# A Mamba block before a mixture of experts on one core: delta spread by 64-row products, padded few-row products, and 26 products of constants a unit on TensorE

## The reference, cut to what matters

```
h = layernorm(x) * gamma + beta
u, z = split(h @ in_proj_w.T)                        # 256 channels each
uc = silu(causal_conv(u, 4 taps) + conv_b)
dt, B, C = split(uc @ x_proj_w.T, [64, 80])          # 64, 16 and 16 columns
delta = softplus(dt @ dt_proj_w.T + dt_proj_b)       # 256 channels
state[d, n] = exp(delta[d] * A[d, n]) * state[d, n] + delta[d] * uc[d] * B[n]   # per time step
y[d] = sum_n state[d, n] * C[n] + uc[d] * D[d]
x = layernorm(x + (y * silu(z)) @ out_proj_w.T + x)
p, e = top2(softmax(x @ Wg + bg))
out = layernorm(x + sum_k p_k * (gelu(x @ W1[e_k] + b1[e_k]) @ W2[e_k] + b2[e_k]))
```

## Time and profile before

| what | value |
|---|---|
| median of 3 runs | 893.62 us (892.45 to 897.2) |
| the profiled execution, its own time | 891.96 us |
| its span, first to last instruction | 890.2 us |
| mean granted clock of TensorE | 0.764 |
| DVE busy | 687.3 us (77% of the span) |
| PE busy | 678.5 us (76%) |
| POOL busy | 530.7 us (60%) |
| ACT busy | 423.3 us (48%) |

### The profile page before, as it was taken

One profiled execution on the slowest core, in us unless ns is written; L12 is line 12 of the kernel. 1 busy time (PEld: TensorE's weight loads), 2 busy tenths in 40 slices (PEclk: granted clock), 3 DMA queues, 4 the chain that ended last, 5 costly groups with the idle time before them and its releaser, 6 DMA issues. The chain is left out here.

```text
span 890.2 us, 12242 instructions
## 1 busy us (share of the span) xinstructions
PE 678.5 (76%) x2905; PEld 311.1 (35%) x2905; DVE 687.3 (77%) x1350; ACT 423.3 (48%) x884; POOL 530.7 (60%) x526
## 2 busy tenths in 40 slices
PE   3768989878778988878888976878631998899920
PEld 2322222222222322222232221212221888888820
DVE  2167788989998897899889899999732677777754
ACT  3537458357465534735655453324110555455424
POOL 5124546745687757677676677867863455455433
PEclk9885867877987776787797666556555899999975
DMA  3074455565376855547465465655003666666646
GB/s 82 0 202 106 95 127 133 121 152 131 82 189 172 196 135 134 122 115 172 105 142 124 112 142 118 161 120 123 24 27 91 166 177 170 176 168 178 181 128 175
DMA packets 60390, 117.37 MB, mean 132 GB/s; under 512 B 8817, under 2 KB 37297, under 8 KB 52257
## 3 DMA queue, kind: packets, MB, share of 16 engines
q1 hardware_dynamic: 56000, 107.60, 49.4%
q0 software_dynamic: 4320, 8.99, 3.1%
HBM read 100.21 MB, written 16.35 MB: 131 GB/s over the span
## 5 line engine op out<-in xcount | busy, mean ns | idle before, releaser
L532 POOL TENSOR_TENSOR hc<-hs,Crep 128x1024 f32<-128x1024 f32 x128 | 300.1, 2355 | 188.2 <-PE bank L759 102.0
L1295 DVE TENSOR_TENSOR_SCAN hs<-bank,state,flow 128x512 f32<-128x512 f32 x256 | 314.6, 1268 | 58.5 <-ACT bank L1061 53.2
L1061 ACT ACTIVATE bank<-bank,negA 128x512 f32<-128x512 f32 x256 | 165.1, 662 | 253.4 <-PE bank L749 242.0
L749 PE MATMUL bank<-delta,sel 32*128 32x512 f32 x512 | 195.0, 839 | 83.3 <-DVE hs L1295 83.2
L1285 DVE TENSOR_TENSOR flow<-flow,bank 128x2048 f32<-128x2048 f32 x63 | 142.7, 2265 | 0.0
L749 PEld LDWEIGHTS bank<-delta,sel 32*128 32x128 f32 x512 | 50.8, 237 | 212.8 <-DVE hs L1295 145.4
L1189 ACT ACTIVATE flow<-bank,b1T 128x128 f32<-128x128 f32 x284 | 81.1, 369 | 79.8 <-PE bank L926 77.6
L759 PE MATMUL bank<-hc,kc 128*32 128x512 f32 x512 | 91.2, 795 | 6.1 <-POOL hc L532 6.1
L698 PE MATMUL bank<-hT,wtapT 128*128 128x512 f32 x128 | 88.9, 822 | 6.9 <-issue 4.9
L926 PE MATMUL bank<-flow 128*128 128x128 f32 x568 | 83.0, 291 | 14.0 <-issue 9.1
L641 POOL DMA_INDIRECT results<-flow,idn x71 | 69.9, 984 | 33.2 <-issue 31.4
(11 more groups left out here) (180 smaller groups left out, 774.8 us busy)
## 6 DMA issues: line engine op xcount, KB each, us to landing
flow<-du_d SPq DMA_DIRECT2D x63, 1024.0 KB, 7.1
flow<-L_ffn_W SPq DMA_DIRECT2D x71, 256.0 KB
xg<-xs SPq DMA_DIRECT2D x71, 66.0 KB
hs<-results SPq DMA_DIRECT2D x16, 256.0 KB, 4.8
du_d<-du SPq DMA_DIRECT2D x28, 128.0 KB, 3.1
xin<-L_attn_x SPq DMA_DIRECT2D x8, 256.0 KB, 3.1
out<-hc SPq DMA_DIRECT2D x8, 256.0 KB, 2.5
results<-flow,idn POOLq DMA_INDIRECT x71
```

The costliest lines, as they stand in the source:

```text
L532: nc.gpsimd.tensor_tensor(hc[:, Q % 2, two, :], hs[:, Q % 2, two, :], Crep[u % 3][:].unsqueeze(1).broadcast_to([P, 2, T]), ALU.mult).then_ ...
L749: ins = nc.tensor.matmul(dbank[i][:], sel[32 * i:32 * i + 32, q % 4, :], delta[u % 2][32 * i:32 * i + 32, q // 4, :])
L1061: nc.scalar.activation(dbank[G % 4][:], dbank[G % 4][:], ACT.Exp, scale=negA[:, ch:ch + 1]).then_inc(s_ex, 1)
L1295: nc.vector.tensor_tensor_scan(hs[:, Q % 2, j, :], dbank[G % 4][:], flow[Q % 3][:, j, :], state[:, Q // QUADS % 2, Q % QUADS, j:j + 1], AL ...
```

## The change

1. `spread_pair` takes 64 rows of delta for each product in place of 32. sel grows from 4 to 2 x 4 matrices, one set for the even and one for the odd groups of 32 rows, with zeros in the rows of the other group. The pair of banks now holds groups 0 and 2, then 1 and 3, so the order of scans within a quad becomes 0, 2, 1, 3 (`ORDER`), and POOL takes tiles 0 and 2, then 1 and 3.
2. `spread_c`, `spread_b` (32 rows) and `proj_dt` (64 rows) use all 96 rows of xdbl, with zeros in the stationary operand where the rows aren't wanted.
3. `spread_b` moves from g=29, ahead of x_proj of unit j+2, to the end of g=31.
4. `c_evac` moves on ACT from g=6 to g=5, ahead of `one_plus` (an activation over 128 x 1024).
5. `keep_busy`: for units j = 1 to 5, at g = 3, 15, 19, 23, 25 and 27, PE issues 4, 3, 6, 3, 4 and 6 products of constant bfloat16 matrices (ones, 128 x 128 by 128 x 512) into the front bank that is filled next. Ahead of them it waits until the fill that was in this bank has been drained: at g=3 by ACT's Relu of the first half of `proj_dt`, at g=19 by `residual` on DVE.
6. The zeros of sel are set by DVE in place of POOL, and DVE also zeroes the unused rows of bcs and wdtT. POOL sets one more constant.

```diff
+ORDER = (0, 2, 1, 3)
+KEPT_BUSY = {3: (4, "dt1", 1), 15: (3, "out", -1), 19: (6, "u1", 2), 23: (3, "z0", 2), 25: (4, "xn", -1), 27: (6, "xn", -1)}
...
-        sel = sb("sel", [P, 4, P])
+        sel = sb("sel", [P, 2, 4, P])
-        wdtT = sb("wdtT", [RANK, HALVES, P])
+        wdtT = sb("wdtT", [XP, HALVES, P])
+        idle_rhs = sb("idle_rhs", [P, T], BF16)
...
 # POOL
-                two = slice(2 * pair, 2 * pair + 2)
+                two = slice(pair, 4, 2)
...
-            link(nc.gpsimd.memset(sel[:], 0.0))
+            pool.wait_ge(s_zero, 6)
             for p in range(4):
-                rows = sel[32 * p:32 * p + 32, :, :].rearrange("r m (n c) -> r m n c", c=CH)
+                rows = sel[32 * p:32 * p + 32, p % 2, :, :].rearrange("r m (n c) -> r m n c", c=CH)
...
+            link(nc.gpsimd.memset(idle_rhs[:], 1.0))
...
 # PE
-            pe.wait_ge(s_k, 8)
+            pe.wait_ge(s_k, 7)
+            pe.wait_ge(s_zero, 6)
...
-                nc.tensor.matmul(o[:], bcs[RANK:XP, 1, :], xdbl[u % 2][RANK:XP, :]).then_inc(s_ff, 1)
+                nc.tensor.matmul(o[:], bcs[:, 1, :], xdbl[u % 2][:]).then_inc(s_ff, 1)
...
-                nc.tensor.matmul(o[:], wdtT[:, h, :], xdbl[u % 2][0:RANK, :]).then_inc(s_ff, 1)
+                nc.tensor.matmul(o[:], wdtT[:, h, :], xdbl[u % 2][:]).then_inc(s_ff, 1)
...
-                nc.tensor.matmul(Brep[:], bcs[RANK:XP, 0, :], xdbl[u % 2][RANK:XP, :]).then_inc(s_br, 1)
+                nc.tensor.matmul(Brep[:], bcs[:, 0, :], xdbl[u % 2][:]).then_inc(s_br, 1)
...
-                q, j = r // 2, 2 * (r % 2)
-                for i in (j, j + 1):
-                    ins = nc.tensor.matmul(dbank[i][:], sel[32 * i:32 * i + 32, q % 4, :],
-                                           delta[u % 2][32 * i:32 * i + 32, q // 4, :])
+                q, odd = r // 2, r % 2
+                for i in range(2):
+                    rows = slice(64 * i, 64 * i + 64)
+                    ins = nc.tensor.matmul(dbank[2 * odd + i][:], sel[rows, odd, q % 4, :], delta[u % 2][rows, q // 4, :])
...
+            def keep_busy(newest, times):
+                drained(pe, newest - 1)
+                for _ in range(times):
+                    nc.tensor.matmul(fbank[(newest + 1) % 2][:], ones[:], idle_rhs[:])
...
-                    if g == 29 and late:
-                        spread_b(j + 1)
...
+                        if g == 31:
+                            spread_b(1)
...
+                    if late and g == 31:
+                        spread_b(j + 1)
+                    if early and g in KEPT_BUSY:
+                        times, what, ahead = KEPT_BUSY[g]
+                        keep_busy(fill_of(j + ahead, what), times)
...
 # ACT
-                ch = tile_of(g // 4, g % 4)
+                ch = tile_of(g // 4, ORDER[g % 4])
...
                         if g == 5:
+                            c_evac(j + 1)
                             one_plus(j + 1)
-                        if g == 6:
-                            c_evac(j + 1)
...
 # DVE
             front_stats(0)
+            nc.vector.memset(sel[:], 0.0).then_inc(s_zero, 1)
+            nc.vector.memset(bcs[0:RANK], 0.0).then_inc(s_zero, 1)
+            nc.vector.memset(wdtT[RANK:XP], 0.0).then_inc(s_zero, 1)
...
-                Q, j = G // 4, G % 4
+                Q, j = G // 4, ORDER[G % 4]
```

More of the change, by code:

```diff
@@ L959, in setup @@
                 nc.scalar.copy(wxpT[:].rearrange("p h c -> p (h c)"), bank[3][:, 0:2 * XP]).then_inc(s_pe, 1)
-                nc.scalar.copy(wdtT[:].rearrange("p h c -> p (h c)"), bank[3][0:RANK, 256:512]).then_inc(s_pe, 1)
+                nc.scalar.copy(wdtT[0:RANK].rearrange("p h c -> p (h c)"), bank[3][0:RANK, 256:512]).then_inc(s_pe, 1)
                 nc.scalar.copy(b1T[:], bank[4][:, 32:64]).then_inc(s_pe, 1)
@@ L1288, in scan @@
             def scan(G):
-                Q, j = G // 4, G % 4
+                Q, j = G // 4, ORDER[G % 4]
                 dve.wait_ge(s_ex, G + 1)
-                if j == 0:
+                if G % 4 == 0:
                     dve.wait_ge(s_bu, Q + 1)
@@ L1400, in _ @@
             nc.vector.tensor_copy(run[:], base).then_inc(s_zero, 1)
-            dve.wait_ge(s_zero, 4)
+            dve.wait_ge(s_zero, 7)
             second_h()
```

## The result

| | changed kernel | kernel before, same chip |
|---|---|---|
| median | 857.28 us (855.64 to 859.91, 4 runs) | 894.91 us (892.45 to 897.2, 4 runs) |
| ratio | 0.9583, 95% interval 0.9545 to 0.9621 | 1 |
| the profiled execution | 859.91 us, span 858.1 | 891.96 us, span 890.2 |
| mean granted clock | 0.872 | 0.764 |

The account below looks back on a forecast made before the run. DVE was taken to bound the units, with 53.2 us of waits for ACT's late decays to win. 29.2 + 5.2 + 1.9 + 0.5 - 4.8 = 32.0 us off 891.96 gave 860.0, median 861.5, range 847 to 884.

Parts of the forecast that it names:

- start, up to the first scan: Before PE's first convolution: POOL's memset of sel leaves the chain it waits for, 0.5 us gained.
- unit 0: Unit 0, wide pairs without constants: half of the 10.3 us of waits besides ACT's silu, 5.2 us gained.
- units 1 to 5, less POOL's meetings: DVE's waits there give 29.2 of 36.9 us; 4.8 lost as `one_hots` is held by POOL, half of four times.
- unit 6: Its longest DVE wait, 1.9 us, gone with the later `spread_b`.
- The signs: DVE's ACT waits about 13 us, units 1 to 5 clock over 0.9, units 68, scan 30's 3.17 gone, over-2-us records.
- 64-row pairs at 1.13 us, padding at nothing: On PE, a 64-row pair costs the same 1.13 us as a 32-row pair at 2.4 GHz; 96 rows cost nothing.
- What goes with a low clock: Narrow products keep PE's clock low; inferred from two stretches, both 81% busy, with clocks 0.80 and 0.50.
- Rival C: Busy time decides the clock: wide pairs do nothing, filled gaps do all; 864.5 us, chance 0.10.
- the move of `spread_b`: At the end of a unit, before scan 30: worth 0.6 us at 1.2 GHz, 3.17 at 2.4 GHz.
- B: In each unit the clock falls before step 19's products and stays low to its end; 879 us, chance 0.15.
- D: The clock stays as it is; the moves give 5.4 us, which POOL takes back; 892 to 893 us, chance 0.11.
- E: PE becomes the bound in units 1 to 5, from 0.47 us per constant product; 906 us, chance 0.09.

Follow-up runs that it names:

- the moves: Kernel before with only B spread later, C copied earlier, new scan order and sel zeros by DVE; no wide pairs, padding or constants: 889.43 us, ratio 0.9954.
- `one_hots` early: Changed kernel with `one_hots` moved from step 0 of the next unit to step 29: 853.39 and 855.33 us; without constants 848.66 us.

## Why the prediction was right

**What bounds the kernel.** Right: the fall of DVE's waits for late decays was the whole gain. They fell by 35.9 us (53.2 to 17.3), DVE's busy time took back 3.8, and the span fell by 32.1.

**The sum, term by term.** Between the first scans, the unit starts and the end:

| term | forecast | measured |
|---|---|---|
| start, up to the first scan | 0.5 gained | 1.0 lost (56.32 to 57.30) |
| unit 0 | 5.2 | 4.6 (75.0 to 70.4, from the first scan); 8.7 when run again (66.3) |
| units 1 to 5, less POOL's meetings | 29.2 - 4.8 = 24.4 | 24.1 (371.7 to 347.6) |
| unit 6 | 1.9 | 4.1 (70.0 to 65.9) |
| unit 7 and after | 0 | 0.3 |

*The start* was right as a mechanism and worth nothing: PE's first convolution begins at 18.75 us and not at 19.42, but its 16 taps then take 10.06 us and not 8.61. Over all kernels here these taps took between 8.55 and 10.11 us and the first scan began between 55.9 and 57.8, whatever was changed; a term of 0.5 us lies under that.

*Units 1 to 5*: DVE's waits came to 8.8 us where 3.7 + 4.0 were left over; behind silu they were 6.4 us for 3.7 (I had put 0.73 a unit, the constants made it 1.05 and in unit 5 2.22), and the rest 2.4 for 4.0. *POOL's meetings*: right in kind, a little small: of the four starts of units 3 to 6, three met POOL (2.57, 2.41 and 2.43 us; the fourth record is 0.44), where I had counted half. `one_hots`' first instruction grew by 8.0 us (5.4 to 13.4) and its second shrank by 2.0 (3.6 to 1.6): 6.0 against 4.8 (when run again, 12.2 and 1.6, it was 4.8). Without constants, moving them took 13.6 us off DVE's work (17.0 to 3.4) and 10 us off the time.

*Unit 6* gained 2.2 us more than forecast, of which 1.8 are DVE's own work (66.65 us busy before, 64.85 after). That is one meeting in the profile of the kernel before, of the kind that the prediction named for `add_log`:

```profile
538.16 2.34 POOL L532 TENSOR_TENSOR hc<-hs,Crep 128x1024 f32<-128x1024 f32 x1
538.23 3.35 DVE L1245 SCALAR_TENSOR_TENSOR delta<-delta,relu 128x1024 f32<-128x1024 f32 x1
```

In the other units this instruction took 1.23 us. In the kernel before with constants, whose unit 6 has none and is the same program, it took 1.23 there too, and the unit 67.5 us for 70.0. So this part of the gain is not the change's, and it hid that the start lost what it was to gain.

*The signs.* Three came: a clock of 0.95, no wait before scan 30, and five records of over 2 us in the line of `one_hots`. Two did not follow from my own sum. It leaves 53.2 - 29.2 - 5.2 - 1.9 = 16.9 us of waits and not 13, and units of 69.5 us and not 68; measured were 17.3 us, and units of 67.4 to 72.3 us. One sign of being wrong came by the letter: DVE waited for B once, 0.7 us at the first `inflow` of unit 1.

**64-row pairs at 1.13 us, padding at nothing.** Right: 1.13 us on the timeline, and 1.12 for the padded B.

**What goes with a low clock.** Right in direction, on thin evidence: the two stretches of the earlier trace rows differ also in how much PE had to do (213 records in 75.0 us, 154 in 64.8), so they could not show that it was the rows. The run with narrow pairs could: with the same instructions, narrow rows gave 0.59 in units 6 and 7 where wide ones gave 0.79. Rival C, that wide pairs do nothing and busy time decides alone, is refuted by that stretch and by the 9 us that narrow pairs cost. Its time nearly holds: the change with narrow pairs still has 27 us of the gain (893.73 to 867.09), close to the 864.5 of that rival, and the moves have only 4 of them by themselves. The other 22 are the constants and the padding, and no run shows in which shares. The Trainium skill (TensorE: Matmul & The Clock Gate, "What's actually happening"), which speaks of how busy PE has been, would put the busier kernel at the higher clock; the runs here show the opposite, 81% busy at 0.59 and 64% at 0.79.

**Where the reasons were incomplete.** Two parts were mis-sized. I gave the high clock to "pairs of 64-row products and full products of constants" together, and counted the constants as hidden. The constants brought no time in any of the three comparisons that take them alone (in the change, in the kernel before, and with `one_hots` early, where the kernel without them is 5 to 7 us faster), and they cost 0.31 us a unit behind silu. And I took the move of `spread_b` as worth 0.6 or 3.17 a unit according to a clock that other edits set. It is worth 13 us beside wide pairs alone, where the clock at the end of the units stays low in three of five, and 22 in the full change, where it also sets the clock there: with B early PE stands still for 4 us and the clock falls. The wide pairs alone and the moves alone brought 0.5% each; together, and with the padding, they bring 3.8% (the kernel without constants), the whole of the gain. Of these 35 us, 17 come only with the padding and the earlier copy of C, in a split that no run shows. That parts which each remove one cause of a late decay leave the other one to be waited for is my reading of this; the waits before scan 30 and at steps 7 to 9 above fit it.

**The other rivals.** B expected the clock to fall at step 19 and stay low: units 1 to 5 ran at 0.95. D is what the moves alone give. E did not come: PE was busy 84% of units 1 to 5, and the constants took 414 ns a record (four in a row 1.04 us from first start to last end), below the 0.47 from which it would have decided.

## What to carry to other kernels

A mean clock is not a time: look at which instructions run slowly just before the wait that ends last, and at what PE stood still for ahead of them, since moving one product that holds the queue can be worth more than any number of products that fill gaps elsewhere. Judge a bundle by its parts in both directions, alone and taken out: here each of the three parts tried alone was worth 0.5% or nothing, and the products of constants could be left out once the pairs were wide. What a part is worth depends on what stands beside it: the constants and the padding, taken out together beside narrow pairs, cost 22 us, and the constants by themselves beside wide pairs nothing. When a bound engine becomes earlier, look for what it now meets on a shared resource, and move the small instruction, not the large one.

## What the runs showed of the hardware that I had not expected

- Two float32 products of 64 rows, one of rows 0 to 63 and one of rows 64 to 127, together take as long as two of 32 rows: 1.13 us at 2.4 GHz, and 2.05 to 2.08 at 1.2.
- At an equal number of products, the rows used go with the granted clock: 0.79 with 64-row pairs and 0.59 with 32-row pairs, in units 6 and 7, which have no constants.
- In the kernel with B early, 4.07 us without work in front of one product were followed by slow products for nearly 6 us, though PE had been at work before: the three groups behind the wait took 2.05, 1.92 and 2.08 us.
- A DVE comparison of 128 x 64 that takes 0.20 us by itself took 2.57 us when a POOL product started 0.13 us after it by the records (2.61 in the kernel before), one of 128 x 32 took 3.07 us, and `add_log`, 1.23 us by itself, 3.35. The Trainium skill (SBUF — State Buffer, "Who interferes with whom") has a DVE instruction with two SBUF inputs exclude a GpSimd one that reads SBUF; the runs agree, and in each of these meetings, whichever record starts first, the DVE instruction was the one held up while POOL's kept its 2.34 or 2.35 us.
